# A recommendation kernel on one core: two more tiles take their eighth field from TensorE, and the layers and last steps change places

## The reference

```
s = jnp.sum(sp_emb, axis=1)
bi_pooled = 0.5 * (s * s - jnp.sum(sp_emb * sp_emb, axis=1))
x = jnp.concatenate([bi_pooled, ds_input], axis=1)
h = jax.nn.relu(x @ w1.T + b1)
h = jax.nn.relu(h @ w2.T + b2)
out = jax.nn.sigmoid(h @ fw.T + fb + lin_output)
```

## Time and profile before

| | |
|---|---|
| median of 3 runs | 400.91 us (400.11 to 402.16) |
| the profiled execution: its time | 398.72 us |
| its span in the trace | 396.9 us |
| busy: PE, VectorE (DVE), ScalarE (ACT), POOL | 378.9, 329.0, 240.3, 287.8 us |
| TensorE's granted clock, mean | 0.993 of full speed |
| matmuls of lines 704 and 707 in the trace | 812 and 812 |

### The profile page before, as it was taken

How to read it: one execution, slowest core, us unless ns; L and a number is a source line. 1 busy time by engine, 2 the same in 40 slices (tenths; PEclk the granted TensorE clock), 3 DMA queues, 4 the chain that set the end, 5 groups by cost and what they waited for, 6 DMA issues and landing times.

```text
span 396.9 us, 5382 instructions
## 1 busy us (share of the span) xinstructions
PE 378.9 (95%) x1766; PEld 324.6 (82%) x1766; DVE 329.0 (83%) x336; ACT 240.3 (61%) x406; POOL 287.8 (73%) x310
## 2 busy tenths in 40 slices
PE   3999999999999999999999999999999988999884
PEld 2888888888888888888888888888888875767542
DVE  6799999979789796997979799697978995485952
ACT  5996865876376673875639756477665465322222
POOL 5777777777777777777777777777777777777740
PEclk9999999999999999999999999999999998999998
DMA  7733236332543327333273223633254222222210
GB/s 226 191 80 29 27 33 184 34 26 14 139 85 27 28 15 194 28 28 29 14 195 27 27 29 43 178 30 26 15 140 69 14 14 14 14 15 14 14 12 0
DMA packets 16900, 23.01 MB, mean 58 GB/s; under 512 B 6084, under 2 KB 15958, under 8 KB 15961
## 3 DMA queue, kind: packets, MB, share of 16 engines
q0 software_dynamic: 9600, 5.09, 22.9%
q1 hardware_dynamic: 7272, 17.58, 13.9%
HBM read 22.60 MB, written 0.04 MB: 57 GB/s over the span
## 4 chain that ended last, share of the span: by engine, by line
PE 92%; DVE 4%; ACT 2%; issue 1%; DMA 1%; ACTq 0%
PE cand L704 42%; PE cand L707 42%; PE bank_b L743 1%; PE bank_b L736 1%; PE bank_b L725 1%; PE bank_b L749 1%; PE bank_b L718 1%; PE bank_b L756 1%; DMA idx_raw<-sparse 1%; DVE sums L420 1%; PE cand L743 1%; PE cand L736 1%; ACT gates L562 1%; DVE last_picks L384 0%; DVE pick_sums L407 0%
## 5 line engine op out<-in xcount | busy, mean ns | idle before, releaser
L301 POOL DMA_INDIRECT rows<-table,row_idx x300 | 286.7, 956 | 94.1 <-issue 70.7
L704 PE MATMUL cand<-high,gates 128*128 128x462 f32 x812 | 308.3, 380 | 0.4 <-DVE gates L352 0.4
L707 PE MATMUL cand<-low,gates 128*128 128x462 f32 x812 | 304.2, 375 | 0.0
L704 PEld LDWEIGHTS cand<-high,gates 128*128 128x128 f32 x812 | 154.4, 190 | 23.2 <-issue 5.0
L707 PEld LDWEIGHTS cand<-low,gates 128*128 128x128 f32 x812 | 154.0, 190 | 20.4 <-issue 2.4
L384 DVE TENSOR_REDUCE picks<-masked 128x66 f32<-128x924 f32 x56 | 107.4, 1917 | 1.9
L378 DVE TENSOR_TENSOR masked<-cand,mask 128x924 f32<-128x924 f32 x57 | 63.7, 1118 | 42.3 <-PE cand L707 42.0
L562 ACT ACTIVATE gates<-distance,one 128x512 fp32r<-128x512 bf16 x116 | 76.9, 710 | 0.0
L554 ACT ACTIVATE distance<-codes,minus_key 128x512 bf16<-128x512 f16 x112 | 74.4, 712 | 0.0
L352 DVE TENSOR_SCALAR gates<-bank_a,key_of 128x512 fp32r<-128x512 f32 x87 | 59.9, 743 | 0.5 <-ACT bank_a L548 0.5
L529 ACT CAST high<-stage 128x462 fp32r<-128x462 f32 (+2 forms) x52 | 31.0, 596 | 33.4 <-DMA stage<-tabs 33.3
(11 more groups left out here) (91 smaller groups left out, 99.1 us busy)
## 6 DMA issues: line engine op xcount, KB each, us to landing
stage<-tabs SPq DMA_DIRECT2D x7, 1617.0 KB
rows<-table,row_idx POOLq DMA_INDIRECT x300, 3.2
codes<-codes_dram SPq DMA_DIRECT2D x28, 128.0 KB, 3.1
stage<-tabs SPq DMA_DIRECT2D x7, 231.0 KB, 4.2
idx_raw<-sparse SPq DMA_DIRECT2D x1, 208.0 KB, 2.5
w_sb<-w2t SPq DMA_DIRECT2D x1, 128.0 KB
xT<-dense_rows SPq DMA_DIRECT2D x1, 120.0 KB
w_sb<-w1x SPq DMA_DIRECT2D x1, 80.0 KB
```

The costliest lines, as they stand in the source:

```text
L301: pool.indirect_dma_start(out=rows[t % RING][:, g * W:(g + 1) * W], out_offset=None, in_=table[:, :], in_offset=bass.IndirectOffsetOnAxis( ...
L704: first = nc.tensor.matmul(to, gate, high[f % 2][:, k, :], start=(k == 0), stop=False)
L707: last = nc.tensor.matmul(to, gate, low[f % 2][:, k, :], start=False, stop=(k == CHUNKS - 1))
```

## The change

Tiles 8 and 9 also take field 7 from TensorE. That makes one more job of two tiles, which stands as job 28, ahead of the job (7, block 3), now job 29; there are 30 jobs, 118 tile lookups instead of 116, and 298 gathers instead of 300. The gates of the two-tile job are 256 wide. Blocks 0 and 1 stay in jobs 26 and 27, block 2 goes into job 29 with step places of its own, `LATE_AT`. In ScalarE's queue the layer-1 relus of a hidden block stand ahead of the second half of the gates. Tile 15's rows are split 13 and 5, and their sums, the turns and the layers behind the jobs are interleaved anew.

```
-    PEF = [MMF - 1, MMF - 1, MMF - 1, MMF]
+    SUMMED = MMF - 1
+    PEF = [MMF if t in (8, 9, 12, 13, 14, 15) else SUMMED for t in range(TILES)]
-    JOBS = [(f, b) for f in range(MMF) for b in range(BLOCKS) if f < PEF[b]]
+    JOBS = [(f, b) for f in range(SUMMED) for b in range(BLOCKS)] + [(SUMMED, BLOCKS - 2), (SUMMED, BLOCKS - 1)]
...
-    SPLIT = GF[LAST] - 3
+    SPLIT = GF[LAST] - 5
...
+    LATE_AT = {(1, 3): TURN, (2, 3): L1A, (2, 6): L1B, (3, 3): L2, (3, 6): L3}
-    HIDDEN = {SUMMED_OF[m] + 2: m for m in range(BLOCKS - 1)}
+    HIDDEN = {SUMMED_OF[0] + 2: 0, SUMMED_OF[1] + 2: 1, NJ - 1: 2}
```

VectorE, behind the jobs:

```
             pick(NJ - 1, 0)
-            sum_pick_squares(BLOCKS - 1)
             dve.wait_ge(gathered[(LAST - 1) % RING], gathered_until(LAST - 1))
             sum_rows(LAST - 1, LAST - 1, 0, GF[LAST - 1])
             pick_last(2)
+            dve.wait_ge(gathered[LAST % RING], gathered_until(LAST) - 16 * (GF[LAST] - SPLIT))
+            sum_rows(LAST, LAST, 0, SPLIT)
             pick_last(3)
             copy_lin(BLOCKS - 1)
             make_x(BLOCKS - 1)
             relu1(BLOCKS - 1, 1)
-            dve.wait_ge(gathered[LAST % RING], gathered_until(LAST) - 16 * (GF[LAST] - SPLIT))
-            sum_rows(LAST, LAST, 0, SPLIT)
```

ScalarE, in the loop over the jobs:

```
+                if j in HIDDEN:
+                    relu1(HIDDEN[j], 0)
                 if j - 1 in SUMMED_OF:
                     square_picks(SUMMED_OF.index(j - 1))
-                if j + 2 < NJ:
+                if j in HIDDEN:
+                    relu1(HIDDEN[j], 1)
+                elif j + 2 < NJ:
                     make_gates(j + 2, FIRST_ACT, ACT_GATES)
```

TensorE, behind the jobs:

```
-            layer2(3)
-            layer3(3)
             pe.wait_ge(y_made, BLOCKS - 1)
             pe.wait_ge(picked, PAIRS + 1)
-            turn(4, LAST, [LAST, LAST + 1]).then_inc(folded, 1)
+            turn_picks(4, LAST)
+            turn_rows(4, LAST, [LAST], LAST + 1)
+            layer2(3)
+            turn_rows(4, LAST, [LAST + 1], LAST + 1).then_inc(folded, 1)
+            layer3(3)
```

More of the change, by code:

```diff
@@ L39, in build_deep_fm @@
     BLOCKS = TILES // TB
-    PEF = [MMF - 1, MMF - 1, MMF - 1, MMF]
-    GF = [F - PEF[t // TB] for t in range(TILES)]
+    SUMMED = MMF - 1
+    PEF = [MMF if t in (8, 9, 12, 13, 14, 15) else SUMMED for t in range(TILES)]
+    GF = [F - PEF[t] for t in range(TILES)]
     GMAX = max(GF)
@@ L65, in build_deep_fm @@
     assert all(h * MUL >> SHIFT == h // J for h in range(J * CHUNKS))
-    JOBS = [(f, b) for f in range(MMF) for b in range(BLOCKS) if f < PEF[b]]
+    JOBS = [(f, b) for f in range(SUMMED) for b in range(BLOCKS)] + [(SUMMED, BLOCKS - 2), (SUMMED, BLOCKS - 1)]
     NJ = len(JOBS)
-    PAIRS = 2 * NJ
+    SIZE = [sum(PEF[t] > f for t in range(b * TB, (b + 1) * TB)) for f, b in JOBS]
+    PAIR = [sum(SIZE[:j]) // 2 for j in range(NJ)]
+    PAIRS = sum(SIZE) // 2
+    FULL = [sum(s == TB for s in SIZE[:j + 1]) for j in range(NJ)]
+    assert SIZE == [TB] * (NJ - 2) + [2, TB]
     CANDS = 3
     FIRST_OF = [min(j for j, (g, b) in enumerate(JOBS) if g == f) for f in range(MMF)]
-    SUMMED = [PEF[b] - ((PEF[b] - 1, b) == JOBS[-1]) for b in range(BLOCKS)]
-    SUMMED_OF = [JOBS.index((SUMMED[b] - 1, b)) for b in range(BLOCKS)]
-    assert JOBS[-1][1] == BLOCKS - 1 and SUMMED_OF == sorted(SUMMED_OF) and SUMMED_OF[-1] == NJ - 2
+    SUMMED_OF = [JOBS.index((SUMMED - 1, b)) for b in range(BLOCKS)]
+    APART = [t for t in range(TILES) if PEF[t] > SUMMED]
+    HALF = SIZE[-2]
     CHUNK_AT = {(FIRST_OF[f - 1] + c // 2, c % 2): (f, c) for f in range(1, MMF - 1) for c in range(CHUNKS)}
     CASTS = {FIRST_OF[MMF - 2] + g: (MMF - 1, g) for g in range(PIECES)}
-    TILE_AT = {2 * t + 2: t for t in range(12)}
-    TILE_AT[26], TILE_AT[27], TILE_AT[28] = 12, 13, 14
+    TILE_AT = {2 * t + 2: t for t in range(TILES - 2)}
+    TILE_AT[NJ - 1] = TILES - 2
     LAST = TILES - 1
-    SPLIT = GF[LAST] - 3
+    SPLIT = GF[LAST] - 5
     def gathered_until(t):
@@ L103, in build_deep_fm @@
     AHEAD = 7
-    LET = [0] + list(itertools.accumulate(19 if j in HIDDEN else 12 for j in range(NJ) for _ in range(TB * len(HALVES))))
+    LET = [0] + list(itertools.accumulate(19 if j in HIDDEN else 12 for j in range(NJ) for _ in range(SIZE[j] * len(HALVES))))
     assert 10 * AHEAD + LET[-1] > 10 * sum(GF)
@@ L351, in make_gates @@
                         dve.wait_ge(gates_used, g - SLOTS + 1)
-                    nc.vector.tensor_scalar(gates[:, g % SLOTS, :], bank_a[:, :], key_of[:, k:k + 1], None,
+                    nc.vector.tensor_scalar(gates[:, g % SLOTS, 0:SIZE[j] * P], bank_a[:, 0:SIZE[j] * P], key_of[:, k:k + 1], None,
                                             ALU.is_equal).then_inc(dve_gates, 1)
@@ L368, in pick @@
                 f, b = JOBS[j]
-                p = 2 * j + h
+                p = PAIR[j] + h
                 t = b * TB + 2 * h
-                if h == 0:
-                    dve.wait_ge(half_matched, j + 1)
+                if h == 0 and SIZE[j] == TB:
+                    dve.wait_ge(half_matched, FULL[j])
                 else:
@@ L382, in pick @@
                 dve.wait_ge(picked, p + 1)
-                to = last_picks[:, 0:2, BOTH] if j == NJ - 1 else picks[:, t:t + 2, f, :]
+                to = picks[:, t:t + 2, f, :]
+                if f == SUMMED:
+                    to = last_picks[:, APART.index(t):APART.index(t) + 2, BOTH]
                 nc.vector.tensor_reduce(to, masked[p % 2][:, :, :].rearrange("p t (s w) -> p t w s", w=W),
@@ L488, in _ @@
                     low_chunk(*CHUNK_AT[j, 0])
-                pick(j, 1)
+                if SIZE[j] == TB:
+                    pick(j, 1)
                 if (j, 1) in CHUNK_AT:
@@ L561, in clip @@
                     act.wait_ge(gates_used, g - SLOTS + 1)
-                nc.scalar.activation(gates[:, g % SLOTS, :], distance[:, k, :], ACT.Relu, bias=one[:, 0:1],
+                nc.scalar.activation(gates[:, g % SLOTS, 0:SIZE[j] * P], distance[:, k, 0:SIZE[j] * P], ACT.Relu, bias=one[:, 0:1],
                                      scale=-1.0).then_inc(act_gates, 1)
@@ L779, in _ @@
             for j in range(1, NJ):
-                for i in range(TB):
-                    p = 2 * j + i // 2
+                at = LATE_AT if j == NJ - 1 else AT
+                for i in range(SIZE[j]):
+                    p = PAIR[j] + i // 2
                     if i % 2 == 0 and p >= CANDS:
@@ L785, in _ @@
                         chunk(j, i, k)
-                        if j in HIDDEN and (i, k) in AT:
-                            m, step = HIDDEN[j], AT[i, k]
+                        if j in HIDDEN and (i, k) in at:
+                            m, step = HIDDEN[j], at[i, k]
                             if step == TURN:
```

62 lines of the change are left out of this document (32 added, 30 removed).

## The result

| | before | changed |
|---|---|---|
| median of 6 executions | 400.83 us (398.73 to 402.16) | 395.38 us (394.89 to 395.81) |
| the profiled execution: its time | 398.72 us | 394.89 us |
| its span in the trace | 396.9 us | 393.1 us |
| mean granted clock of TensorE | 0.993 | 1.0 |
| matmuls of lines 704 and 707, now 718 and 721 | 812 and 812 | 826 and 826 |

The ratio is 0.9862, with a 95% interval of 0.9841 to 0.9884: 5.5 us faster, 1.4%. I had forecast 398.0 us, 0.7% faster, with 396.3 as the lower end. The direction and the mechanism hold and the size does not. The two profiled executions are 3.8 us apart, the medians 5.5 us.

The account below looks back on a forecast made before the run. TensorE's queue was taken as the bound, with POOL close. Terms gave +0.42 us up to tile 12's turn and -3.3 at the end: -2.9 on 398.72, or 395.8; with the median's 2.2 us carried over, 398.0 us, range 396.3 to 400.8.

Parts of the forecast that it names:

- The wait in job 26: TensorE's L1B of block 0 no longer waits for ScalarE's first relu: -3.07 us.
- The slow clock behind it: TensorE's matmuls after L1B in job 26 no longer run at 1.2 GHz: -1.70 us, bounds 0 and 1.70.
- My rival: Clock drop after job 26's wait absent from ordinary runs: gain only 1.2 us, 399.7 us; chance 0.14.
- The carried-over 2.2 us: Median's distance above the profiled execution (400.91 against 398.72 us), added unchanged to the forecast.
- The work added: On TensorE, 28 lookup matmuls (+5.88 us) and two more turning pairs (+0.44 us), hidden by nothing.
- block 2: Layer 2 of block 2 no longer waits for ScalarE's second relu: -1.23 us.
- Job 27: L1B of block 1 waits slightly for ScalarE's relu: +0.1 us, bounds 0 and 3.07.
- The rival that put the wait there: Late relu at L1B of block 1, job 27; a 3.5 us wait gives a median of 403.1 us; chance 0.06.
- VectorE in job 29: VectorE finishes picks and sums at 381.3 us, before its tiles 12 to 14 step at 382.2: margin 0.9 us.
- The end: Tile 15's earlier sums bring its last turning pair to 387.9 us; -3.3 us, bounds 0 and 3.6.
- POOL: Two gathers fewer: last starts at 379.2 us, lands at 382.5, margin nearly 3 us; POOL waits only for its own issue.
- The two lookups: Two more tile lookups in TensorE's queue, 28 matmuls at 0.21 us: +5.88 us, part of the 6.3 us added.

Follow-up runs that it names:

- the run with the relus first: Kernel before with only ScalarE's order changed: layer-1 relus ahead of the squared picks and the second half of the gates; median 394.65 us, ratio 0.9826.
- the run with the old order: Changed kernel with ScalarE's old order in jobs 26 and 27, squared picks and all gates ahead of the relus; median 402.82 us, ratio 1.0046.

## Why the prediction was wrong in size and right in mechanism

*The wait in job 26* (-3.07): right. L1B starts at 325.84, the last matmul ahead of it at 325.63, and the run with the relus first shows it alone.

*The slow clock behind it* (-1.70, bounds 0 and 1.70): this is the term that failed. It was read right from one trace, but taken for a constant of the kernel, with itself as the upper bound. Most executions of the kernel before have a lower mean clock than that one. In the one of 400.57 us that was traced the term is 3.10 us, and 0.94 us more are lost at the end. My rival said that the drop might be absent elsewhere, and put its chance on a smaller gain. The rule of the Trainium skill that I set beside it ("TensorE: Matmul & The Clock Gate", Part 1, a window that runs freely) fits what was then measured: one and the same 3 us wait cost 1.70 us in one execution and 3.10 in another. I drew only one of its two consequences: that the gain may be smaller, not that it may be larger.

*A low clock at the end* was not in the sum at all, and I wrote that the rows show the drop once. The same trace shows it a second time (windows of PE):

```profile
394.00:397.00 3.00, 0.64 (x3) 0.56 0.00 0
```

There it costs 0.22 us: from the last layer 3 to the last sigmoid 0.63 us, in the changed kernel 0.41.

*The carried-over 2.2 us.* The sum was made for an execution of 398.72 us and the distance to the median, 400.91, was added again at the end. I took it for something that the change leaves alone. In the execution of 400.57 us it is low clock: 1.40 us behind the wait in job 26, which went with the wait, and 0.94 us in the last steps, where the changed kernel's trace shows a clock of 1.0 (with the relus alone 0.66 us of that kind were left). With both added to the terms, the sum is -2.9 - 2.3 = -5.2 us, or 395.7 us; measured 395.38.

*The work added* (+6.32) and *block 2* (-1.23): right. From the turn of block 0 to that of tile 12 the changed kernel takes 60.66 us, where the kernel before took 60.54; the sum said 0.42 us more, 0.12 was measured. The 0.30 us between them lie mostly in how I read the two waits: counted from one start to the next, less the usual 0.21 us, they cost 3.23 and 1.38 us and not 3.07 and 1.23. Everything before job 26 happened to be 0.38 us sooner in the changed kernel's execution; that is the start again (first matmul of 0.37 us at 11.40 us, in the kernel before at 12.21), and luck.

*Job 27* (+0.1): 0.17 us. The rival that put the wait there had its place right and its size wrong; the run with the old order shows what it would have been, 3.31 us and the clock, 402.8 us.

*VectorE in job 29* (margin 0.9 us): it stood idle for 0.91 us before the first step for tiles 12 to 14.

```profile
381.63 0.56 DVE L445 COPY xT<-bank_a 1x384 f32<-1x384 f32 x1 [0.91 <-PE bank_a L746]
```

*The end* (-3.3): from the turn of tile 12 to the last sigmoid 15.47 us before and 391.34 - 379.41 = 11.93 now, -3.54. Right in the change, but not by itself: the end alone brings 1.2 us, because with 300 gathers it waits for POOL and then for a slow TensorE. I had named what two gathers fewer save POOL (2.5 us) only as a margin of the last sums, and not seen that the first sums, now ahead of the last pick, need it.

*POOL.* Its margin was right (last gather at 378.96 us, forecast 379.2), but it does not wait for its own issue alone: 67 further waits, 20.4 us in all, are for TensorE's matmuls. Each is 0.3 us too, so its pace is the same.

*The two lookups.* I booked them as a cost of 6.3 us that the rest pays back. That is right along TensorE's queue, and misses that this end, as it stands, needs them: without them the same kernel takes 4.0 us more, since TensorE only waits for the gathers, at the price of its clock.

What the change is worth thus comes from its relus (6.0 us alone). The remainder, lookups, block 2's place and the end, is worth about nothing on top: 0.9826 for the relus alone, 0.9862 and 0.9871 for all, the last on another chip. The traces show why: it costs 4.99 us between the turn of block 0 and that of tile 12 (55.67 us for the relus alone, 60.66 for all) and gives 4.21 us back behind it (16.14 and 11.93).

## What to carry to other kernels

When single executions of a kernel differ, sort them by the granted clock before predicting from one of them: a wait of about 3 us on TensorE had cost here the wait and 1.7 to 3.1 us more, and a sum made on one of the fastest executions leaves this out. An order that frees one engine is worth nothing where another's pace, here POOL's 1.25 us a gather, then releases the step; look for what is late next with the new order, not with the old. Where TensorE must wait, matmuls whose results nobody reads can shorten the kernel: 2.6 us in job 26 here. For the shorter waits at the end the runs do not show it clearly (395.31 us with fillers, 395.22 without).

## What was unexpected about the hardware

A wait of 3.0 us was followed by 1.2 GHz until somewhere near 333 us in one execution and into the stretch from 333 to 336 us in another of the same program, so the price of one wait takes several values. With the last steps' 0.94 us it makes up the difference between the two traced groups (398.6 and 400.6 us); those near 400.0 and 402.1 us were not traced. Idleness of 1.1 and 1.2 us within the jobs left the clock alone in the traces read here, while 1.3 us behind the turn of tile 14 were followed by 0.66 in one traced execution of the changed kernel (a second has the same mean clock, 0.996), and the other ten have a mean clock of 1.0. At the start the matmuls leave the low clock at 11.1 us in one execution and at 14.2 us in another, and the clock column does not show it. Fourteen matmuls without a use, put into a wait, made a kernel 2.6 us faster.
